# A mask written by ScalarE in the attention stack, and parted loads and stores in the expert layers

## What is computed

```python
x = attn_layer(shift_tokens(x), Wqkv, q_scale, k_scale, Wo) + x
    # q, k: l2norm, scale, rotary; then per window, over its own and the former window's keys
    mask = (it < jb) | (it > jb + w) | (jb == -1)
    sim = jnp.einsum('bhwie,bhwje->bhwij', bq, bk2) * 8.0
    sim = jnp.where(mask, -jnp.finfo(sim.dtype).max, sim)
    out = jnp.einsum('bhwij,bhwje->bhwie', jax.nn.softmax(sim, -1), bv2)
x = ffn_layer(shift_tokens(x), ...) + x        # layer norm, 128 -> 2 x 341, a * gelu(gate), 341 -> 128

assign = jnp.argmax(x @ centroids.T, axis=-1)  # one of E = 8 experts for each of the 2048 tokens
y = disp + relu(layernorm(disp) @ W1[e] + b1[e]) @ W2[e] + b2[e]     # 128 -> 512 -> 128
```

## Time and profile before

| | |
|---|---|
| median of 3 runs | 5264.44 us (5263.94 to 5267.1) |
| the profiled execution | 5258.44 us, its span 5256.6 us |
| mean granted clock of TensorE | 0.95 |
| TensorE matmul / weight load busy | 4483.1 us (85%) / 3044.1 us (58%) |
| VectorE / ScalarE / GpSimd busy | 2962.2 (56%) / 3004.0 (57%) / 3092.2 us (59%) |
| DMA queue of SP | 352.86 MB, 23.3% of 16 engines |
| chain that ended last | PE 41%, ACT 20%, issue 10%, DVE 10%, DMA 5%, SP's queue 3% |

### The profile page before, as it was taken

The page is one execution under the profiler, slowest core; times in us unless marked ns, Lnnn a source line. Parts: engine busy times, 40 slices in busy tenths (PEclk is TensorE's granted clock), DMA queues, the critical chain, the costliest instruction groups (busy, mean ns, idle before and its releaser), DMA issues.

```text
span 5256.6 us, 114135 instructions
## 1 busy us (share of the span) xinstructions
PE 4483.1 (85%) x40863; PEld 3044.1 (58%) x41275; DVE 2962.2 (56%) x5398; ACT 3004.0 (57%) x6559; POOL 3092.2 (59%) x1906
## 2 busy tenths in 40 slices
PE   7878999999999999868999999999999834489965
PEld 4556666666666666636666666666666612345544
DVE  5666666666666666536666666666666543055521
ACT  4546666666666666636666666666666622145531
POOL 1118777777777777608777777777777632111111
PEclk9999999999999999989999999999999966789986
DMA  1002232323323232302232323323232201200012
GB/s 59 0 0 86 83 101 82 98 83 93 89 82 100 82 98 82 85 9 84 85 100 82 97 83 94 88 83 100 82 95 84 74 0 35 72 3 0 0 41 73
DMA packets 349584, 364.21 MB, mean 69 GB/s; under 512 B 58737, under 2 KB 285042, under 8 KB 348786
## 3 DMA queue, kind: packets, MB, share of 16 engines
q1 hardware_dynamic: 346994, 352.86, 23.3%
q0 software_dynamic: 2048, 4.20, 0.3%
HBM read 247.13 MB, written 109.71 MB: 68 GB/s over the span
## 4 chain that ended last, share of the span: by engine, by line
PE 41%; ACT 20%; issue 10%; DVE 10%; DMA 5%; SPq 3%; POOL 2%; ACTq 0%; DVEq 0%; POOLq 0%
PE banks L315 5%; PE banks L354 5%; PE banks L281 4%; PE banks L310 4%; PE banks L294 3%; ACT arena L449 3%; ACT arena L435 3%; DVE arena L522 3%; DVE arena L519 3%; DMA v_rows<-arena 3%; PE banks L409 2%; PE banks L415 2%; PE banks L846 2%; PE banks L371 2%; DMA arena<-in_moe_w 2%
## 5 line engine op out<-in xcount | busy, mean ns | idle before, releaser
L623 POOL TENSOR_TENSOR arena<-arena 128x512 f32<-128x512 f32 x768 | 962.1, 1274 | 778.6 <-DVE arena L552 663.3
L628 POOL TENSOR_TENSOR arena<-arena 128x1024 f32<-128x1024 f32 x384 | 907.0, 2362 | 30.1
L625 POOL TENSOR_TENSOR arena<-arena 128x1024 f32<-128x1024 f32 x384 | 906.0, 2359 | 0.0
L426 ACT ACTIVATE arena<-arena 128x512 f32<-128x512 f32 x384 | 242.2, 631 | 943.9 <-DVE arena L522 943.9
L545 DVE TENSOR_REDUCE arena<-arena 128x8 f32<-128x512 f32 x768 | 491.3, 680 | 492.4 <-ACT arena L444 492.4
L310 PE MATMUL banks<-w_qk,arena 128*128 128x512 f32 x1536 | 731.6, 599 | 30.2 <-DVE arena L655 25.2
L552 DVE SCALAR_TENSOR_TENSOR arena<-arena,banks 128x512 f32<-128x512 f32 x768 | 493.4, 684 | 282.9 <-ACT arena L462 282.9
L294 PE MATMUL banks<-arena 128*32 128x128 f32 x12288 | 433.4, 275 | 80.0 <-ACT arena L468 75.9
L281 PE MATMUL banks<-arena 128*32 128x128 f32 x12288 | 429.3, 277 | 62.3 <-issue 7.4
L315 PEld LDWEIGHTS banks<-w_v,arena 128*128 128x128 f32 x1536 | 268.2, 190 | 348.6 <-ACT arena L435 314.4
L315 PE MATMUL banks<-w_v,arena 128*128 128x256 f32 x1536 | 425.8, 400 | 43.7 <-ACT arena L435 28.4
(11 more groups left out here) (205 smaller groups left out, 7706.4 us busy)
## 6 DMA issues: line engine op xcount, KB each, us to landing
v_rows<-arena SPq DMA_DIRECT2D x1536, 64.0 KB, 2.1
arena<-v_rows SPq DMA_DIRECT2D x768, 128.0 KB, 2.5
arena<-v_rows SPq DMA_DIRECT2D x768, 112.0 KB, 2.4
arena<-in_moe_w SPq DMA_DIRECT2D x30, 515.5 KB, 3.7
w_qk<-in_stack_qk SPq DMA_DIRECT2D x48, 256.0 KB, 3.0
w_v<-in_stack_v SPq DMA_DIRECT2D x48, 128.0 KB, 3.3
w_o<-in_stack_o SPq DMA_DIRECT2D x12, 512.0 KB, 3.7
w_w<-in_stack_w SPq DMA_DIRECT2D x12, 341.0 KB, 3.3
```

Of the source, the lines that this page charges most:

```text
L623: nc.gpsimd.tensor_tensor(f.sined[:, :, :, half, :], x[:, :, :, 1 - half, :], sines[:, :, mine].unsqueeze(1).to_broadcast([D, GH, 4, DH // ...
L625: nc.gpsimd.tensor_tensor(rot, x.rearrange("p h t a d -> p h t (a d)"), cosines.unsqueeze(1).to_broadcast([D, GH, 4, DH]), ALU.mult).then_ ...
L628: nc.gpsimd.tensor_tensor(rot, rot, f.sined.rearrange("p h t a d -> p h t (a d)"), ALU.add).then_inc(S.rotated, 1)
```

## The change

In the stack the mask is no longer a matmul. ScalarE copies it into bank 4 once ahead of the stack, and then in every step right after Exp of unit s-3, which comes after VectorE has read the bank, for the next unit's scores. It signals `masked`, for which TensorE waits ahead of the scores; these go on adding to what stands in the bank. `q_turned` and `k_turned` become one semaphore, `heads_turned`, that counts two a unit.

In the expert layer there are five slots instead of three. SP only loads: for tile i it waits for a free slot and for load i-2, and issues the weights, then the rows. The weights of the first tile are issued ahead of the wait for the scatter. Even and odd tiles have a landing semaphore each. ScalarE issues the store of a tile itself, right after its copy, once the copy is done and the store before has landed. `logits` and `counted` become one semaphore.

```diff
@@ -273,7 +273,8 @@
         u = s - 3
         st.wait(S.heads_taken, u + 1)
         st.wait(S.shifted, u)
-        pe.matmul(scores, M.identb[:], M.wmask[:], start=True, stop=False, skip_group_check=True)
+
+        pe.wait_ge(S.masked, st.n + (u + 1 + st.call))
         sv = scores.rearrange("p (t h k) -> p t h k", t=2, h=2)
         for win in range(NW):
             c = 32 * (win % 4)
@@ -370,7 +371,7 @@
             o = hp * T + tile * 128
             last = pe.transpose(bank(M, 2 if qk else 3)[:, o:o + 128],
                                 f.rot[:, u % 2, 2 * tile + qk, 2 * hp:2 * hp + 2, :], M.ident[:])
-    last.then_inc(S.k_turned if qk else S.q_turned, 1)
+    last.then_inc(S.heads_turned, 1)
 
 
 def pe_stack_hidden(M, st, place):
@@ -424,12 +425,13 @@
         st.wait(S.probs_turned, u)
         st.wait(S.summed, u)
         nc.scalar.activation(f.p, f.zs, ACT.Exp, scale=8.0).then_inc(S.probs, 1)
+        nc.scalar.copy(bank(M, 4), M.wmask[:]).then_inc(S.masked, 1)
     if st.on(2):
         u = s - 2
-        st.wait(S.q_turned, u + 1)
+        st.wait_twice(S.heads_turned, 2 * u + 1)
         st.wait(S.scores, u - 1)
         nc.scalar.copy(f.q[:, u % 2].rearrange("p h t -> p (h t)"), bank(M, 3))
-        st.wait(S.k_turned, u + 1)
+        st.wait_twice(S.heads_turned, 2 * u + 2)
         for par in range(2):
             r = slice(64 * par, 64 * par + 64)
             last = nc.scalar.copy(f.kbd[r, u % 2, :, par, WIN:WIN + T],
@@ -614,7 +616,7 @@
         if st.new_layer and s == 0:
             pool.wait_ge(S.tables, st.layer + 1)
         st.wait(S.scaled, u + 1)
-        st.wait(S.k_turned, u - 1)
+        st.wait_twice(S.heads_turned, 2 * u - 2)
         st.wait(S.rotated, u)
         x, rot = f.qn[:, u % 2], f.rot[:, u % 2].rearrange("p t h d -> p h t d")
         cosines, sines = (f.tab[:, i].rearrange("p (t d) -> p t d", t=4) for i in range(2))
@@ -636,6 +638,7 @@
 
 def act_stack(M, act, m):
     act.wait_ge(M.st.zeroed, m.k + 1)
+    M.nc.scalar.copy(bank(M, 4), M.wmask[:]).then_inc(M.st.masked, 1)
     unit_steps(M, act, m, act_stack_step)
     act.wait_ge(M.st.state, 1 + 4 * DEPTH * (m.k + 1))
 
@@ -1120,7 +1123,7 @@
 
 MT = 256
 MOE_TILES = N // MT + E_X - 1
-SLOTS = 3
+SLOTS = 5
 W_ROW = F_X + 4 * D + 4 + 3
 PICKS = 22
 
@@ -1140,12 +1143,19 @@
     return w[:, 0:F_X], w[:, F_X:o].rearrange("p (c d) -> p c d", c=4), w[:, o:o + 4], w[:, o + 4:o + 7]
 
 
+def moe_loaded(S, k, i):
+
+    if i % 2:
+        return S.loaded_odd, 32 * (MOE_TILES // 2 * k + i // 2 + 1)
+    return S.loaded_even, 32 * ((MOE_TILES + 1) // 2 * k + i // 2 + 1)
+
+
 def pe_moe(M, pe, m):
     S, w, f, k = M.mo, M.w, moe_buffers(M), m.k
     gate = bank(M, 7, 16 * E_X).rearrange("p (t e) -> p t e", e=E_X)
     for t in range(16):
         last = pe.matmul(gate[:, t, :], M.z[:, t * 128:t * 128 + 128], w.cent[:], start=True, stop=True)
-    last.then_inc(S.logits, 1)
+    last.then_inc(S.counted, 1)
     ln_pe(M, pe, M.z, 4 * m.ln_inner)
     pe.wait_ge(S.pick, PICKS * k + 7)
     pe.wait_ge(M.s.ln_log, 4 * m.ln_inner + 4)
@@ -1175,7 +1185,7 @@
                     last.then_inc(S.first, 1)
         i = step + 1
         if i < MOE_TILES:
-            pe.wait_ge(S.loaded, 32 * (n + i + 1))
+            pe.wait_ge(*moe_loaded(S, k, i))
             if i >= 1:
                 pe.wait_ge(S.normed, n + i)
             for h in range(2):
@@ -1234,9 +1244,12 @@
         if i >= 2:
             j = i - 2
             act.wait_ge(S.y_turned, n + j + 1)
-            if j >= 2:
-                act.wait_ge(S.stored, 16 * (n + j - 1))
             nc.scalar.copy(f.yt[:, j % 2].rearrange("p h d -> p (h d)"), bank(M, 7, MT)).then_inc(S.y_copied, 1)
+            act.wait_ge(S.y_copied, n + j + 1)
+            if n + j:
+                act.wait_ge(S.stored, 16 * (n + j))
+            act.dma_start(M.sorted_out[j * MT:j * MT + MT].rearrange("(h p) d -> p h d", h=2),
+                          f.yt[:, j % 2]).then_inc(S.stored, 16)
 
 
 def dve_moe(M, dve, m):
@@ -1345,25 +1358,18 @@
     S, w, f, k = M.mo, M.w, moe_buffers(M), m.k
     n = MOE_TILES * k
     sp.wait_ge(S.pick, PICKS * (k + 1))
-    for i in range(MOE_TILES + 3):
-        if i < MOE_TILES:
-            if i == 0:
-                sp.wait_ge(S.scattered, 16 * 16 * (k + 1))
-            if i >= 1:
-                sp.wait_ge(S.loaded, 32 * (n + i))
-            if i >= SLOTS:
-                sp.wait_ge(S.y_taken, n + i - SLOTS + 1)
-            e = sp.value_load(w.owner[0:1, i:i + 1], min_val=0, max_val=E_X - 1)
-            sp.dma_start(f.xs[:, i % SLOTS], M.sorted_in[i * MT:i * MT + MT].rearrange("(h p) d -> p h d", h=2)
-                         ).then_inc(S.loaded, 16)
-            sp.dma_start(f.w[:, i % SLOTS], M.ins["moe_w"][bass.ds(e * D, D)]).then_inc(S.loaded, 16)
-        j = i - 3
-        if j >= 0:
-            sp.wait_ge(S.y_copied, n + j + 1)
-            if j >= 1:
-                sp.wait_ge(S.stored, 16 * (n + j))
-            sp.dma_start(M.sorted_out[j * MT:j * MT + MT].rearrange("(h p) d -> p h d", h=2),
-                         f.yt[:, j % 2]).then_inc(S.stored, 16)
+    for i in range(MOE_TILES):
+        e = sp.value_load(w.owner[0:1, i:i + 1], min_val=0, max_val=E_X - 1)
+        if i >= SLOTS:
+            sp.wait_ge(S.y_taken, n + i - SLOTS + 1)
+        if i >= 2:
+            sp.wait_ge(*moe_loaded(S, k, i - 2))
+        sem = S.loaded_odd if i % 2 else S.loaded_even
+        sp.dma_start(f.w[:, i % SLOTS], M.ins["moe_w"][bass.ds(e * D, D)]).then_inc(sem, 16)
+        if i == 0:
+            sp.wait_ge(S.scattered, 16 * 16 * (k + 1))
+        sp.dma_start(f.xs[:, i % SLOTS], M.sorted_in[i * MT:i * MT + MT].rearrange("(h p) d -> p h d", h=2)
+                     ).then_inc(sem, 16)
 
 
 def pe_program(M, pe):
...
```

More of the change, by code:

```diff
@@ L1251, in dve_moe @@
     nc.vector.memset(f.upto[:, :, 0:4], 0.0)
-    dve.wait_ge(S.logits, k + 1)
+    dve.wait_ge(S.counted, 2 * k + 1)
     nc.vector.tensor_copy(f.lg, gate).then_inc(S.pick, 1)
@@ L1275, in dve_moe @@
     ln_dve_scale(M, dve, M.xc, 4 * m.ln_inner)
-    dve.wait_ge(S.counted, k + 1)
+    dve.wait_ge(S.counted, 2 * k + 2)
     nc.vector.tensor_tensor(f.over, shares.unsqueeze(2).to_broadcast([D, E_X, E_X]),
@@ L1437 @@
 STACK_SIGNALS = """w_group0 w_group1 w_group2 w_group3 w_o w_scales w_ffn tables zeroed padded tokens qk
- squared lengths logged inverse scaled spun rotated q_turned k_turned heads_taken scores
+ squared lengths logged inverse scaled spun rotated heads_turned heads_taken masked scores
  maxed shifted probs summed inverted probs_turned probs_taken v v_taken v_stored v_loaded outs normed outs_turned
@@ L1445 @@
 LEAD_SIGNALS = "projected qkv prod reduced step shifted exped att turned at out_projected residual"
-MOE_SIGNALS = """logits pick counted rows_turned rows_taken scattered loaded turned normed first relu second
+MOE_SIGNALS = """counted pick rows_turned rows_taken scattered loaded_even loaded_odd turned normed first relu second
  y_taken y_turned y_copied stored gathered returned residual"""
```

## The result

The changed kernel takes 5294.36 us (median of 5 runs, 5287.3 to 5300.21); the kernel before, on the same chip, 5264.44 (5262.89 to 5271.21). The ratio is 1.0053 [1.0038, 1.0067]: slower by 30 us, where 77 us faster was forecast, and outside the forecast's range. The profiled execution took 5292.06 us, its span 5290.3, against 5256.6 before. First the page: span, busy shares, and the chain that ended last by engine.

What follows compares the result with a forecast made beforehand. It took a TensorE, scores, VectorE, ScalarE, v loop to bound the stack, and waits on loads and stores the expert loop. 5258.4 + 55 - 132 = 5181.4, with the median's 6.0 offset 5187 us; 8-in-10 range 5138 to 5240.

Steps and rivals of the forecast that it cites:

- What bounds the kernel: Stack: a loop of TensorE, scores, VectorE, ScalarE (Exp, q, k), v; v waits for the k copies in 378 of 384.
- Copy ahead of q: Stack, ScalarE: the mask copy between Exp and the q copy delays what follows by 0.50 us, bounds 0.47 and 0.60.
- Cover in two of eight steps: Stack steps 1 and 6: TensorE's extra work hides some 0.2 us of the copy, so 96 units pay 0.
- I take 0.30: Stack, TensorE: removing the mask's weight load and matmul saves 0.30 us in each of 384 units, bounds 0.10 to 0.30.
- From v to the next scores TensorE alone sets the time: Stack loop: only TensorE's work counts between v and the next scores; used with the 0.30 us matmul saving.
- Copy and removal together: Both stack stages: copy cost and matmul saving net +58 us, rounded to +55; bounds +25 and +173.
- Rival 2: Stack: a 0.60 us copy with only 0.10 won back costs +192 us, 5324 in all, slower; chance 0.08.
- Experts: Expert loops: waits gone, 4.5 us a tile, 63 us between first and last transpose, -132 us; bounds -147 and -117.
- Rival 1: Expert loops: two loads in flight only share DMA engines, 5.06 us interval stays, 117 us saved, 5202; chance 0.18.
- Rival 3: Expert loops: TensorE's clock stays low, a pass takes 7.9 us, only 36 us saved, 5283; chance 0.05.
- rival 4: Stack: ScalarE's idle 2.5 us hides the copy, so the stack gains 115 us, 5017 in all; chance 0.04.

Runs made afterwards that it cites:

- e4: Kernel before plus ScalarE's mask copy after Exp and its wait, with the mask matmul kept and overwriting the copy: 5465.82 us, ratio 1.0383.
- e3: Kernel before with the mask matmul removed and no copy in its place, so it computes something else: 5248.02 us, ratio 0.9963.
- after: The changed kernel with both parts, stack and expert layers, against the kernel before: 5294.36 us, ratio 1.0053.
- e7: Kernel before with the expert change alone, mask matmul kept, but each load waits for the one before to land: 5125.46 us, ratio 0.9731.
- e11: Changed kernel plus a one-column matmul where the mask matmul stood: 5272.55 us, ratio 1.0013 to the kernel before.

## Why the prediction was wrong

**What bounds the kernel: right.** v waits for the k copies, in 378 of 384 units before and after. **Copy ahead of q: right in size**, 0.50 forecast, 0.51 in the timeline, 0.52 by e4. The figures of the Trainium skill ("ScalarE: Activation LUTs", What ACT_TABLE_LOAD costs) had given an estimate of 0.52 us, and the trace agrees with its 0.51.

**Cover in two of eight steps: wrong.** I let 96 units pay 0.30 less, since v starts up to 0.2 us after the k copies there. That cover is at v only. In the 11.27 us step the last pair of L415 waits for ScalarE's L498 (it adds a bias in the hidden layer), which stands behind the same copies; before, then after:

```profile
1579.81 1.09 PE L415 MATMUL banks<-xc,w_w 128*85 128x512 f32 x2 [0.45 <-ACT xc L498]
```

```profile
1637.06 1.09 PE L416 MATMUL banks<-xc,w_w 128*85 128x512 f32 x2 [0.72 <-ACT xc L500]
```

What v hid comes back there: from Exp to these matmuls it is 5.81 us before and 6.33 after, 0.52 more. The copy costs 384 x 0.52 = 200 us, where my terms make 288 x 0.50 + 96 x 0.30 = 173: 27 us.

**"I take 0.30": the step that failed.** I credited every unit with 0.30 us for the removed matmul, 115 us in all, and bounded it at 0.10 from below. Three things were wrong with it. Its size is 0.21: the transposes stand 0.53 us ahead of the scores without it, not the 0.44 that I took from transposes ahead of other transposes. It counts only where TensorE's arrival releases Exp; in half of the steps VectorE's queue, led by the hidden layer, does. The table gives 0.8 us in eight steps, 0.10 a unit, or 38 us. And the edges of the layers give some 20 of these back: about 18 us are left, which is e3's median (in its trace the stack stages are 12 us shorter). That is 97 us of the error, and with the 27 above 124 of the stack's 128. The prediction argued "From v to the next scores TensorE alone sets the time", and never looked from the scores to Exp in the steps with hidden-layer work, where L519's missing idle time stood in the trace.

Copy and removal together: +200 - 38 + 20 = +182, measured +183; forecast +55. That the three terms meet the measured sum so closely is partly luck, as each is good to a few us. Rival 2 named this ("the mask's copy costs more than it frees, and decides"); it asked for 0.34 us net a unit, the kernel has 183 / 384 = 0.48. Its 0.10 us won back a unit is what the table gives; its copy of 0.60 was too dear, and with the experts at -150 it would have come to about 5306.

**Experts: right, a little small.** -150 against -132. A tile takes 3.9 us, the dense pass of the earlier trace rows, not 4.5, as the clock is low only in the first passes (the 3.78 us above): 55 and 57 us from first to last transpose instead of 63 make about 14 of the 18. **Rival 1 fell:** the loop does not keep the interval of 5.06 us, neither in after (3.9) nor in e7 (4.2), where only one tile's loads are under way. The rule of the Trainium skill behind it ("DMA: Bandwidth & Descriptors", Issuing engines are not separate DMA queues) says that DMAs of several engines interleave and that only issue time is saved. The store's landing fits the first half: 1.8 us before and in e7, 3.7 where it runs beside the next loads. The rows' 4.0 us does not speak for it, as it is 3.6 in e7 too, where they stand behind their own weights. The second half doesn't hold for this kernel as a whole: a store that waited for ScalarE stood in SP's queue ahead of a load, and parting them gave 41 us with three slots. **Rival 3 fell** (clock 0.95 in the loop's first 55 us), **rival 4 too**: ScalarE's 2.5 us stand before Exp still.

## What to carry to other kernels

A saving on one engine is worth something only in the steps in which that engine releases the next link; look at each kind of step for the queue with no idle time before it, and credit the saving there alone. A cost on a chain that others wait for was paid here in every step, and a cover seen at one consumer did not hold for the next one behind the same queue. Where an operation has to be added, put it on the engine whose queue has room between its own waits: the same copy cost 200 us on ScalarE behind Exp, and on VectorE nothing that could be measured.

## What was not expected of the hardware

TensorE stands still where the hardware loop jumps back, and for how long, and between which of its instructions, changes with how many it has: in the first stack 3.4 to 3.8 us ahead of the scores in after, 3.1 to 3.5 in e3, 0.4 to 0.7 us in e11 with one more matmul, of one column, in each unit; in the second stack 2.0 to 2.5 us in the middle of the scores in after and e3. The one matmul was worth 17 and 22 us of a kernel. TensorE goes on 1.2 to 1.5 us after an instruction transfer of 16 KB has landed, which points to its code as what it waits for; no run tests that.
